# Weights handed over input dimension first in a graph and expert kernel

## The chip, the core and the metric
The program runs on one core of one Trainium2 chip as a single launch. The metric is the device time of that launch in microseconds (us); weights may be laid out in another order on the host before the launch, and that is not part of it. TensorE multiplies matrices, VectorE and ScalarE work elementwise, GpSimd issues the transfers that need an index per row (gathers and scatters) and SyncE issues the plain ones. Sixteen DMA engines carry both kinds. Each engine runs its own list of instructions in order, and semaphores are all that orders one list against another.

## The reference
The input is 6250 nodes of 512 numbers and 100000 edges (`src`, `dst`). Four layers follow each other, each on the layer-normalised result of the last and each added back to it: two narrow graph convolutions with a layer norm between them; a gated feed-forward layer with weights rounded to three levels; a third graph convolution; and 16 experts, one per token, chosen by a router.

```python
agg = segment_sum(x[src], dst); deg = maximum(segment_sum(1, dst), 1)     # third convolution
agg = agg / deg[:, None]
x3 = x + alpha * (agg @ W.T + b)                                          # W: 512 x 512
...
logits = xf @ switch_w.T + switch_b                                       # router, 16 x 512
probs = softmax(logits); routes = argmax(probs); route_probs = max(probs)
pos = running count of the route so far;  capacity = int(1.2 * N / 16)    # 468
buf[routes, pos] = xf                                                     # where pos < capacity
y = einsum('ecd,efd->ecf', buf, expert_w) + expert_b                      # expert_w: 16 x 512 x 512
out = where(pos < capacity, y[routes, pos], xf) * route_probs
```

All three weights (`W`, `switch_w`, `expert_w`) stand with the output dimension first. The product sums over the input dimension, and TensorE sums over the 128 partitions of its two operands, so it needs both with the input dimension on the partitions.

## The kernel before, in words
The program has four stages one after the other, with a barrier between them. The first sorts out edges, the second prepares tables, the third does the first two convolutions and the feed-forward layer, and the fourth, which is the one changed (from L1764 on), does the third convolution, the router and the experts. In every stage each engine has one function that issues its instructions in a written-out order (`@block.tensor`, `@block.scalar` and so on).

*Head of the fourth stage.* SyncE loads `Wg` into `wg`, the router's weights into `sw` (16 partitions of 512) and some small things. TensorE turns `Wg` in four groups of four 128x128 transposes into PSUM (L2081), and ScalarE copies each group into `wgT` (L2261); four more transposes and a copy make `swT`. Meanwhile VectorE clears 29 of 49 blocks of the sums `agg` (L2399), and ScalarE the rest. `wg` serves afterwards as the space of two other tiles (`scaled`, `xf`).

*Third convolution.* GpSimd gathers rows of the edges by unit (L1971); VectorE builds one-hot matrices (L2435); TensorE sums rows into nodes (L2122); ScalarE scales; TensorE turns the sums (L2140) and multiplies by `wgT` (L2150). Layer norm, logits (L2170) and routing tables follow a few tiles behind in the same loop.

*Experts.* Each of 16 experts has 468 slots, in tiles of 128, 128, 128 and 84 rows: 64 tiles, numbered f. For a tile, GpSimd has gathered the rows (`gather`, L1979) two experts ahead into `er`; ScalarE normalises them into `xe` (L2331); TensorE turns them (`turn_rows`, L2206); ScalarE rounds the turned rows to the narrower fp32 format of TensorE into `erT` (L2338), and VectorE keeps the remainder (L2552). The product (L2217) takes 12 matmuls of 512 columns: high part times high part, remainder times high, high times remainder, over four blocks of 128 inputs. VectorE adds the bias (L2595) and the scaled residual (L2597), and GpSimd scatters the result to `out` (L1996). The expert's weights go the same way as the rows: loaded into `we` (two buffers, L2043), turned (`turn_weights`, L2198) into `pWT`, rounded by ScalarE (`copy_weights`, L2325) and split by VectorE (`weights_rest`, L2547) into `weT`. While tile m of expert e is multiplied, block m of the weights of expert e+1 goes through these steps. In TensorE's order that is, per tile: rows of the next tile, a block of the next expert's weights, the product of this tile.

*What holds what.* SyncE loads the weights of expert e over those of e-2 when TensorE has turned the latter (L2069), and its next bias when the tiles of e-2 are finished (`biased`); both waits stand in one list. Before the first scatter, GpSimd waits for seven last blocks of `out` that SyncE stores after the gather of expert 0 has landed (L1993, L2065).

Of the kernel before, what the change touches and what calls it, by code (L numbers as in the profile page):

```python
# [4 lines left out]
F32 = mybir.dt.float32  # L5
# [11 lines left out]
P = 128  # L17
N = 6250
D = 512
DK = D // P  # L20
# [49 lines left out]
NX = 16  # L70
# [297 lines left out]
def program(nc, x, src, dst, node_vec, W1, b1, gamma, beta, W2, b2, w_gate, w_up, w_down,  # L368
            alpha, Wg, bg, switch_w, switch_b, expert_w, expert_b, out):
    with ExitStack() as whole:  # L370
# [889 lines left out]
        with ExitStack() as ctx:  # L1260
# [507 lines left out]
            "loaded loads const bg3 wT_ps wT scaled aT_ps aT conv res x3 var std rs xf xT_ps xT logits lg_done lg expd onehot cum placed "  # L1768
# [4 lines left out]
        es = {n: sem("e_" + n) for n in "wT_ps wT wT_lo xe xT_ps xT xT_lo y_ps biased y".split()}  # L1773
# [6 lines left out]
        with ExitStack() as ctx:  # L1780
# [18 lines left out]
            wg = sb(ctx, "wg", [P, DK, D], F32)  # L1799
# [9 lines left out]
            scaled, xf = wg[:, 0:2, :], wg[:, 2:4, :]  # L1809
# [3 lines left out]
            sw = aT[0:NX, 0].rearrange("p a b -> p (a b)")  # L1813
# [30 lines left out]
            pWT = [pb(ctx, f"pWT{j}", [P, DK, P], F32) for j in range(2)]  # L1844
# [159 lines left out]
            def _(sp):  # L2004
                sp.dma_start(wg[:], Wg.rearrange("(m p) d -> p m d", p=P)).then_inc(s["w_in"], 16)
                sp.dma_start(res[0:3, 0, :], bg.partition_broadcast(3)).then_inc(s["bias_in"], 16)
                sp.dma_start(alp[:], alpha.partition_broadcast(P)).then_inc(s["small_in"], 16)
                sp.dma_start(sw, switch_w).then_inc(s["small_in"], 16)
# [33 lines left out]
                def load_weights(e):  # L2042
                    sp.dma_start(we[:, e % 2, :, :], expert_w[e].rearrange("(m p) d -> p m d", p=P)).then_inc(ew_in[e % 2], 16)  # L2043
# [24 lines left out]
                for e in range(2, NX):  # L2068
                    sp.wait_ge(es["wT_ps"], (e - 1) * DK)  # L2069
                    load_weights(e)  # L2070
                    sp.wait_ge(es["biased"], (e - 1) * ET)
                    load_bias(e)

            @block.tensor
            def _(pe):
                pe.wait_ge(s["w_in"], 16)
                for c in range(DK):
                    if c > 0:
                        pe.wait_ge(s["wT"], c)
                    for m in range(DK):  # L2080
                        last = nc.tensor.transpose(pW[:, m * P:(m + 1) * P], wg[:, m, c * P:(c + 1) * P], ident[:])  # L2081
                    last.then_inc(s["wT_ps"], 1)
                pe.wait_ge(s["small_in"], 48)
                for c in range(DK):
                    last = nc.tensor.transpose(pT[:, 0, c * NX:(c + 1) * NX], sw[:, c * P:(c + 1) * P], ident[0:NX, 0:NX])
                last.then_inc(s["wT_ps"], 1)
                pe.wait_ge(s["wT"], DK + 1)
# [55 lines left out]
                def convolve(i, k):  # L2143
                    T = i * G + k
                    if isinstance(i, int) and T == 0:
                        pe.wait_ge(s["bg3"], 1)
                    wait_alone(pe, s["aT"], T + (1 + FREE), s["fence_pe"])
                    wait_alone(pe, s["x3"], T + FREE, s["fence_pe"])
                    for c in range(DK):
                        nc.tensor.matmul(pW[:], aT[:, k % 2, c, :], wgT[:, c, :], start=(c == 0), stop=False)  # L2150
                    nc.tensor.matmul(pW[:], tri[0:3, 1, :], bg3[:], start=False, stop=True).then_inc(s["conv"], 1)
# [40 lines left out]
                def turn_weights(e, c):  # L2192
                    if c == 0:
                        pe.wait_ge(ew_in[e % 2], (e // 2 + 1) * 16)
                    if e * DK + c >= 2:
                        pe.wait_ge(es["wT_lo"], e * DK + c - 1)
                    for m in range(DK):
                        last = nc.tensor.transpose(pWT[c % 2][:, m, :], we[:, e % 2, m, c * P:(c + 1) * P], ident[:])  # L2198
                    last.then_inc(es["wT_ps"], 1)

# [39 lines left out]
                turn_weights(0, 0)  # L2240
                turn_weights(0, 1)
                fill(G - 1, None)
                turn_weights(0, 2)
                turn_weights(0, 3)
                turn_rows(*experts[0])
                for f, e, m, n in experts:
                    if f + 1 < len(experts):
                        turn_rows(*experts[f + 1])
                    if e + 1 < NX:
                        turn_weights(e + 1, m)  # L2250
                    product(f, e, m, n)

            @block.scalar
            def _(act):
# [4 lines left out]
                for c in range(DK):  # L2259
                    act.wait_ge(s["wT_ps"], c + 1)  # L2260
                    nc.scalar.copy(wgT[:, c, :], pW[:]).then_inc(s["wT"], 1)  # L2261
                act.wait_ge(s["wT_ps"], DK + 1)
                nc.scalar.copy(swT[:].rearrange("p a b -> p (a b)"), pT[:, 0, 0:DK * NX]).then_inc(s["wT"], 1)

# [121 lines left out]
            def _(dve):  # L2386
# [248 lines left out]

_INS = ['x', 'src', 'dst', 'node_vec1', 'L0_gnn_W1', 'L0_gnn_b1', 'L0_gnn_gamma', 'L0_gnn_beta', 'L0_gnn_W2',
# [21 lines left out]
```

## Time and profile before

| what | value |
|---|---|
| median of 3 timed runs | 3362.64 us (3353.38 to 3371.6) |
| profiled execution, first to last instruction (its span) | 5135.2 us |
| mean granted clock of TensorE in it | 0.765 of full speed |
| fourth stage in it | from 3387.3 us |
| routing of the last tiles, between convolution and experts | about 4842 to 4894 us |
| experts (first to last product) | 4894.4 to 5128 us |
| busy, TensorE / VectorE / ScalarE / GpSimd | 2982.4 / 1973.4 / 1285.4 / 2000.5 us |

The profiled execution lies far above the timed ones; its own time is known as its span only. In the rows below PE is TensorE (its matmuls and transposes) and PEld its loading of the stationary operand, DVE is VectorE, ACT ScalarE, POOL GpSimd and SPq the transfers that SyncE issues. A timeline row gives the start in us from the beginning of the span, the duration in us, engine, line and operation, what is written and read with its shape, the number of instructions run together, and in brackets how long the engine was idle before and what ended that ("issue" means that nothing seen in the profile did). A row of a group ends with busy us and mean ns of one, and the idle time before. A row of a stretch gives from:to, its length, the busy us and number of instructions of PE, PEld, DVE, ACT and POOL, the granted clock, the DMA engines' busy share and GB/s. A row of a tile gives the count, the shortest, median and longest duration in ns, and the first and last start.

### The profile page before, as it was taken

What the parts mean: (1) busy time and instruction counts of PE and PEld (TensorE: products, weight loads), DVE (VectorE), ACT (ScalarE), POOL (GpSimd) and SP (SyncE); (2) the same over time, 40 slices, a digit from 0 to 9 for tenths busy, and PEclk for the clock granted to TensorE, in tenths of its full rate; (3) what the DMA queues carried; (4) which work ended last, traced back from release to release, by engine and by line L of the source; (5) the groups of instructions that cost most, each with busy time, mean ns of one, the idle gap of its engine ahead of it and who ended that gap; (6) DMA issues with size and microseconds to landing.
All of it is one profiled execution on the core that took longest, in us unless ns stands there. A gap on an engine that the chain in (4) does not pass through costs nothing. (4 is left out here: it accounts for less than half of the span.)

```text
span 5135.2 us, 61590 instructions
## 1 busy us (share of the span) xinstructions
PE 2982.4 (58%) x17153; PEld 2061.9 (40%) x17154; DVE 1973.4 (38%) x3813; ACT 1285.4 (25%) x2086; POOL 2000.5 (39%) x2038
## 2 busy tenths in 40 slices
PE   7511179631111000299989999956667666665789
PEld 7400068620000000177777777732232232322477
DVE  9300079750000000166666566632223223232366
ACT  3200057410000000144444444420011111111344
POOL 0377700037777777300000000035555455554244
PEclk9555589755555555599999999977888788887799
DMA  3101023210000000022333233345555556555465
GB/s 101 39 5 11 4 64 96 61 41 3 3 3 3 3 3 3 6 91 88 107 95 102 88 104 100 100 151 168 168 170 161 163 173 182 170 161 158 134 193 155
DMA packets 241523, 466.48 MB, mean 91 GB/s; under 512 B 77093, under 2 KB 107069, under 8 KB 241235
## 3 DMA queue, kind: packets, MB, share of 16 engines
q0 software_dynamic: 107264, 235.06, 17.4%
q1 hardware_dynamic: 133970, 227.93, 14.2%
q8 instruction: 138, 2.26, 0.2%
q14 instruction: 151, 1.23, 0.1%
HBM read 395.90 MB, written 73.45 MB: 91 GB/s over the span
## 5 line engine op out<-in xcount | busy, mean ns | idle before, releaser
L1971 POOL DMA_INDIRECT rows<-xn_rows,srcT x784 | 744.2, 949 | 665.4 <-DVEq L2441 440.7
L129 POOL DMA_INDIRECT msg_c<-hid_rows,srcT x744 | 770.0, 1035 | 245.0 <-issue 236.5
L2122 PE MATMUL pV<-rows,oh 128*128 x2240 | 645.5, 435 | 331.6 <-issue 262.2
L2122 PEld LDWEIGHTS pV<-rows,oh 128*128 x2240 | 238.7, 107 | 724.1 <-issue 576.2
L1197 PE MATMUL pG<-parts,los 128*128 128x200 bf16 x2640 | 308.6, 258 | 322.7 <-issue 322.7
L1487 PE MATMUL gates<-xT,wgu_hi 128*128 128x384 f32 (+1 forms) x1848 | 472.3, 377 | 39.2 <-ACT gate_sum L1585 20.6
L1954 POOL IOTA bases<- 128x49 f32 x1 | 0.2, 188 | 1269.8 <-POOLq L387 1269.8
L1518 PE MATMUL accs<-wd,hT 128*128 128x512 f32 x1617 | 405.4, 398 | 16.2 <-DVE hT L1733 16.2
L129 POOL DMA_INDIRECT msg_b<-hid_rows,srcT x344 | 345.5, 1004 | 110.2 <-issue 105.6
L1197 PEld LDWEIGHTS pG<-parts,los 128*128 128x128 bf16 x2640 | 240.9, 100 | 356.0 <-issue 354.2
L1487 PEld LDWEIGHTS gates<-xT,wgu_hi 128*128 128x128 f32 x1848 | 336.4, 190 | 105.4 <-issue 60.9
L1518 PEld LDWEIGHTS accs<-wd,hT 128*128 128x128 f32 x1617 | 303.5, 189 | 88.1 <-issue 28.4
L2435 DVE SCALAR_TENSOR_TENSOR oh<-ids,bases,dstT 128x896 f32 x160 | 184.1, 1150 | 401.4 <-issue 375.8
L2423 DVE TENSOR_TENSOR agg<-agg,pV x161 | 110.1, 684 | 547.9 <-PE pV L2122 348.2
L994 DVE TENSOR_REDUCE picked<-pG 128x32 f32<-128x800 f32 x110 | 108.5, 987 | 462.2 <-remote 359.4
L1433 PE MATMUL accs<-parts_c,los_c 128*128 128x200 bf16 x168 | 47.7, 323 | 305.0 <-issue 304.9
L2273 ACT ACTIVATE wg<-agg,invdeg 128x512 f32 (+1 forms) x49 | 35.3, 721 | 701.7 <-DVEq L118 578.6
L2150 PE MATMUL pW<-wgT,aT 128*128 128x512 f32 x392 | 197.4, 651 | 18.8 <-issue 12.6
L2217 PE MATMUL pY<-weT,erT 128*128 128x512 f32 (+1 forms) x768 | 193.7, 401 | 3.2 <-DVE weT L2547 2.2
L1637 DVE TENSOR_REDUCE msg_c<-accs 128x32 f32<-128x800 f32 x7 | 6.9, 991 | 485.2 <-remote 485.2
L1467 PE MATMUL accs<-w2b,aggT 128*128 128x512 f32 x8 | 8.2, 1125 | 290.1 <-issue 162.2
L1346 POOL MEMSET msg_c<- 128x152 f32 x1 | 0.2, 225 | 447.8 <-POOLq L387 447.8
(432 smaller groups left out, 5300.1 us busy)
## 6 DMA issues: line engine op xcount, KB each, us to landing
wd<-wd_rows SPq DMA_DIRECT2D x154, 512.0 KB
we<-in_L_ffn_expert_w SPq DMA_DIRECT2D x16, 1024.0 KB
lo<-lo_rows SPq DMA_DIRECT2D x110, 128.0 KB
x_rows<-xr SPq DMA_DIRECT2D x49, 256.0 KB, 4.0
xn_rows<-pair SPq DMA_DIRECT2D x49, 256.0 KB
rows<-xn_rows,srcT POOLq DMA_INDIRECT x784
res<-x_rows SPq DMA_DIRECT2D x49, 256.0 KB
x_rows<-agg SPq DMA_DIRECT2D x49, 256.0 KB
```

The lines of the kernel that those rows point to most:

```text
L129: nc.gpsimd.indirect_dma_start(msg[:, c, :], None, table, bass.IndirectOffsetOnAxis(ap=srcT[:, c:c + 1], axis=0)).then_inc(landed[u % 2], 16)
L994: nc.vector.tensor_reduce(picked[:, g // MB % 2, 4 * (g % MB):4 * (g % MB) + 4, :].rearrange("p (b c) f -> p b (c f)", b=2), pG[g % AHEAD] ...
L1197: last = nc.tensor.matmul(into, los[:, g % AHEAD, b, k * P:(k + 1) * P], parts[:, j, b].rearrange("p f h -> p (f h)"), start=False, stop=( ...
L1433: last = nc.tensor.matmul(into, los[:, g % AHEAD, b, k * P:(k + 1) * P], parts[:, j, b].rearrange("p f h -> p (f h)"), start=False, stop=( ...
L1487: last = nc.tensor.matmul(ps[:, 0:n], w, v, start=(m == 0), stop=(m == len(terms) - 1))
L1518: last = nc.tensor.matmul(acc4[j][:], h, wd[:, slot, w, :], start=(f == 0 and m == 0), stop=(f == FB - 1 and m == 2))
L1971: nc.gpsimd.indirect_dma_start(rows[:, u % RING, c, :], None, xn2_rows, bass.IndirectOffsetOnAxis(ap=srcT[:, u * Q + c:u * Q + c + 1], axi ...
L2122: last = nc.tensor.matmul(pV[:, ds(to, 1), :].rearrange("p a d -> p (a d)"), oh[:, ds(to, 1), c, :].rearrange("p a d -> p (a d)"), rows[:, ...
L2150: nc.tensor.matmul(pW[:], aT[:, k % 2, c, :], wgT[:, c, :], start=(c == 0), stop=False)
L2217: last = nc.tensor.matmul(pY[f % 2][0:n, :], erT[:, f % 2, j, c, 0:n], weT[:, e % 2, k, c, :], start=(j, k, c) == terms[0], stop=(j, k, c) ...
L2423: nc.vector.tensor_tensor(at, at, pV[:, ds((v + 1) % 2, 1), :].rearrange("p a b -> p (a b)"), ALU.add).then_inc(s["added"], 1)
L2435: nc.vector.scalar_tensor_tensor(oh[:, ds(v % 2, 1)].rearrange("p a q n -> p (a q) n"), bc(ids.unsqueeze(1), (P, Q, P)), bases[:, ds(tile, ...
```

## The change
The host hands over `W` and `switch_w` transposed and `expert_w` with its last two dimensions exchanged. SyncE loads the first two straight into `wgT` and `swT` (the latter now 128 partitions with four runs of 16 numbers each), and the head of the stage has no transposes and no copies of them. The space of `wg` remains as `between`, and the PSUM of `pWT` remains reserved. In the experts `turn_weights` is gone: ScalarE rounds from `we` itself and waits for its load, VectorE takes the remainder from `we`, and SyncE waits for VectorE's remainder before it loads over a buffer. TensorE's waits for the two loads of the head stand before its first convolution.

```diff
@@ SyncE, head and experts
-                sp.dma_start(wg[:], Wg.rearrange("(m p) d -> p m d", p=P)).then_inc(s["w_in"], 16)
+                sp.dma_start(wgT[:], WgT.rearrange("(c p) d -> p c d", p=P)).then_inc(s["w_in"], 16)
-                sp.dma_start(sw, switch_w).then_inc(s["small_in"], 16)
+                sp.dma_start(swT[:], switch_wT.rearrange("(c p) n -> p c n", p=P)).then_inc(s["small_in"], 16)
-                    sp.dma_start(we[:, e % 2, :, :], expert_w[e].rearrange("(m p) d -> p m d", p=P)).then_inc(ew_in[e % 2], 16)
+                    sp.dma_start(we[:, e % 2, :, :], expert_wT[e].rearrange("(c p) d -> p c d", p=P)).then_inc(ew_in[e % 2], 16)
                 for e in range(2, NX):
-                    sp.wait_ge(es["wT_ps"], (e - 1) * DK)
+                    sp.wait_ge(es["wT_lo"], (e - 1) * DK)
                     load_weights(e)
@@ TensorE, head
-                pe.wait_ge(s["w_in"], 16)
-                for c in range(DK):
-                    if c > 0:
-                        pe.wait_ge(s["wT"], c)
-                    for m in range(DK):
-                        last = nc.tensor.transpose(pW[:, m * P:(m + 1) * P], wg[:, m, c * P:(c + 1) * P], ident[:])
-                    last.then_inc(s["wT_ps"], 1)
...
-                pe.wait_ge(s["wT"], DK + 1)
                 pe.wait_ge(s["const"], 1)
                 pe.wait_ge(s["added"], 1)
@@ TensorE, convolve
                     if isinstance(i, int) and T == 0:
                         pe.wait_ge(s["bg3"], 1)
+                        pe.wait_ge(s["w_in"], 16)
+                        pe.wait_ge(s["small_in"], 48)
@@ TensorE, experts
-                def turn_weights(e, c):
-                    if c == 0:
-                        pe.wait_ge(ew_in[e % 2], (e // 2 + 1) * 16)
-                    if e * DK + c >= 2:
-                        pe.wait_ge(es["wT_lo"], e * DK + c - 1)
-                    for m in range(DK):
-                        last = nc.tensor.transpose(pWT[c % 2][:, m, :], we[:, e % 2, m, c * P:(c + 1) * P], ident[:])
-                    last.then_inc(es["wT_ps"], 1)
...
                 for f, e, m, n in experts:
                     if f + 1 < len(experts):
                         turn_rows(*experts[f + 1])
-                    if e + 1 < NX:
-                        turn_weights(e + 1, m)
                     product(f, e, m, n)
@@ ScalarE, experts
                 def copy_weights(e, c):
-                    act.wait_ge(es["wT_ps"], e * DK + c + 1)
+                    if c == 0:
+                        act.wait_ge(ew_in[e % 2], (e // 2 + 1) * 16)
                     if e >= 2:
                         act.wait_ge(es["y_ps"], (e - 1) * ET)
-                    nc.scalar.copy(weT[:, e % 2, 0, c, :], pWT[c % 2][:].rearrange("p a b -> p (a b)")).then_inc(es["wT"], 1)
+                    nc.scalar.copy(weT[:, e % 2, 0, c, :], we[:, e % 2, c, :]).then_inc(es["wT"], 1)
@@ VectorE, experts
-                    nc.vector.tensor_tensor(weT[:, e % 2, 1, c, :], pWT[c % 2][:].rearrange("p a b -> p (a b)"),
+                    nc.vector.tensor_tensor(weT[:, e % 2, 1, c, :], we[:, e % 2, c, :],
@@ host
+TURNED = {'L1_gnn_W': (1, 0), 'L1_ffn_switch_w': (1, 0), 'L1_ffn_expert_w': (0, 2, 1)}
```

On TensorE, at the border between the last but one and the last expert, these instructions stand in the order of before (`pWT` is the PSUM of the turned weights, `pXT` that of the turned rows, `pY` the product):

```order
L2206 MATMUL pXT<-ident,xe 128x128 x4
L2198 MATMUL pWT<-ident,we 128x128 x4
L2217 MATMUL pY<-weT,erT 84x512 x12
L2206 MATMUL pXT<-ident,xe 128x128 x4
L2217 MATMUL pY<-weT,erT 128x512 x12
```

and in the changed one:

```order
L2186 MATMUL pXT<-ident,xe 128x128 x4
L2197 MATMUL pY<-weT,erT 84x512 x12
L2186 MATMUL pXT<-ident,xe 128x128 x4
L2197 MATMUL pY<-weT,erT 128x512 x12
```

The four transposes of the weights are gone from every tile of the first 15 experts; the last expert had none before. On TensorE between routing and the first product stood (`pS` takes the counts and tables of the routing):

```order
L2179 MATMUL pS<-oh16b,tri 128x112 x2
L2198 MATMUL pWT<-ident,we 128x128 x8
L2186 MATMUL pS<-names,slot 128x128 x7
L2198 MATMUL pWT<-ident,we 128x128 x8
L2206 MATMUL pXT<-ident,xe 128x128 x8
L2198 MATMUL pWT<-ident,we 128x128 x4
L2217 MATMUL pY<-weT,erT 128x512 x12
```

and now stands:

```order
L2168 MATMUL pS<-oh16b,tri 128x112 x2
L2175 MATMUL pS<-names,slot 128x128 x7
L2186 MATMUL pXT<-ident,xe 128x128 x8
L2197 MATMUL pY<-weT,erT 128x512 x12
```

Twenty transposes are gone there; ScalarE and VectorE keep their instructions in their places and read `we` in place of `pWT`.

## Rows read from the trace of the kernel before

**Rows 1.** The page's costliest groups, TensorE's sums of the third convolution.
```profile
L2122 PE MATMUL pV<-rows,oh 128*128 x2240 | 645.5, 435 | 331.6 <-issue 262.2
```

**Rows 2.** Busy time by stretch, middle of the experts.
```profile
5000.00:5050.00 50.00, 50.00 (x280) 41.01 (x279) 35.95 (x57) 24.75 (x42) 27.69 (x28) 1.00 0.69 200
```

**Rows 3.** Timeline, TensorE's weight loads over one tile.
```profile
5004.29 0.58 PEld L2206 LDWEIGHTS pXT<-ident,xe 128*128 128x128 f32 x4
5004.85 0.47 PEld L2198 LDWEIGHTS pWT<-ident,we 128*128 128x128 f32 x4
5005.28 2.60 PEld L2217 LDWEIGHTS pY<-weT,erT 128*128 128x128 f32 x12
...
5007.92 0.52 PEld L2206 LDWEIGHTS pXT<-ident,xe 84*128 84x128 f32 x4
```

**Rows 4.** Timeline, the same in the last expert.
```profile
5115.74 0.59 PEld L2206 LDWEIGHTS pXT<-ident,xe 128*128 128x128 f32 x4
...
5118.94 0.59 PEld L2206 LDWEIGHTS pXT<-ident,xe 128*128 128x128 f32 x4
```

**Rows 5.** Timeline, start of the experts, up to tile 8.
```profile
4909.71 1.03 POOL L1996 DMA_INDIRECT out<-ye,index  x1 [12.48 <-issue]
...
4911.27 0.65 PE L2198 MATMUL pWT<-ident,we 128*128 128x128 f32 x4 [0.71 <-DMA we<-in_L_ffn_expert_w]
...
4919.94 0.82 ACT L2331 ACTIVATE xe<-er 128x512 f32<-128x512 f32 x1 [3.71 <-DMA er<-x_rows,index]
...
4921.40 0.59 PEld L2206 LDWEIGHTS pXT<-ident,xe 128*128 128x128 f32 x4
...
4929.78 2.99 PE L2217 MATMUL pY<-weT,erT 128*128 128x512 f32 x12 [2.15 <-DVE weT L2547]
```

**Rows 6.** Instructions on the tile pWT.
```profile
L2325 ACT CAST weT<-pWT x64: 586/594/607, 4874.6 to 5113.5; 128x512 fp32r<-128x512 f32 x64
L2547 DVE TENSOR_TENSOR weT<-pWT,weT x64: 675/679/692, 4885.0 to 5114.6; 128x512 fp32r<-128x512 f32 x64
```

**Rows 7.** Timeline of the third stage, a remainder out of SBUF.
```profile
3383.04 0.69 DVE L1754 TENSOR_TENSOR pair<-xn,pair 128x512 f16<-128x512 f32 x1 [2.45 <-ACT pair L1615]
```

**Rows 8.** Timeline, VectorE and GpSimd over one tile.
```profile
5001.13 0.69 DVE L2595 TENSOR_TENSOR ye<-pY,be 84x512 f32<-84x512 f32 x1 [0.95 <-issue]
5001.15 0.97 POOL L1981 DMA_INDIRECT er<-x_rows,index  x1 [0.30 <-issue]
...
5001.85 0.75 DVE L2597 SCALAR_TENSOR_TENSOR ye<-ye,er 84x512 f32<-84x512 f32 x1
...
5003.12 0.68 DVE L2547 TENSOR_TENSOR weT<-pWT,weT 128x512 fp32r<-128x512 f32 x1
...
5004.77 0.69 DVE L2595 TENSOR_TENSOR ye<-pY,be 128x512 f32<-128x512 f32 x1 [0.97 <-issue]
```

**Rows 9.** Timeline, SyncE's issue of an expert's weights.
```profile
5002.22 0.44 SPq L2043 DMA_DIRECT2D we<-in_L_ffn_expert_w  x1
```

**Rows 10.** Busy time by stretch, ten microseconds after that load.
```profile
5012.50:5013.00 0.50, 0.50 (x5) 0.34 (x4) 0.47 (x2) 0.50 (x2) 0.50 (x1) 1.00 0.01 0
```

**Rows 11.** SyncE's waits: total us, times, longest us.
```profile
SPq L2046 <- DVE ye L2595: 176.2, 13, 18.5
...
SPq L118 <- DMA x_rows<-tok: 4.2, 2, 2.1
```

**Rows 12.** Timeline, head of the fourth stage.
```profile
3392.16 12.43 DVE L2399 MEMSET agg<- 128x14848 f32 x1 [3.16 <-issue]
...
3405.24 0.21 ACT L2263 COPY swT<-pT 128x64 f32<-128x64 f32 x1 [1.01 <-issue]
...
3412.75 1.15 DVE L2435 SCALAR_TENSOR_TENSOR oh<-ids,bases,dstT 128x896 f32 x1 [3.05 <-issue]
```

**Rows 13.** Instructions on the tile ye, 4930 to 5115 us.
```profile
L2597 DVE SCALAR_TENSOR_TENSOR ye<-ye,er x52: 746/752/753, 4930.3 to 5113.3; 128x512 f32<-128x512 f32 x39, 84x512 f32<-84x512 f32 x13
```

**Rows 14.** Instructions on the tile er, 4930 to 5115 us.
```profile
L1981 POOL DMA_INDIRECT er<-x_rows,index x50: 956/976/1276, 4930.6 to 5105.5; - x50
```

More of the change, by code:

```diff
@@ L368, in program @@
 def program(nc, x, src, dst, node_vec, W1, b1, gamma, beta, W2, b2, w_gate, w_up, w_down,
-            alpha, Wg, bg, switch_w, switch_b, expert_w, expert_b, out):
+            alpha, WgT, bg, switch_wT, switch_b, expert_wT, expert_b, out):
     with ExitStack() as whole:
@@ L1767, in program @@
             "w_in small_in bias_in fence fence_sp fence_pe fence_dve fence_act rows_ready rows_used oh_ready mm_done added whole "
-            "loaded loads const bg3 wT_ps wT scaled aT_ps aT conv res x3 var std rs xf xT_ps xT logits lg_done lg expd onehot cum placed "
+            "loaded loads const bg3 scaled aT_ps aT conv res x3 var std rs xf xT_ps xT logits lg_done lg expd onehot cum placed "
             "mapped map_ps map_free z tok_out tok_free indexed blank cleared dve pool".split())}
@@ L1772, in program @@
         o_out = [sem(f"d_o_out{k}") for k in range(G)]
-        es = {n: sem("e_" + n) for n in "wT_ps wT wT_lo xe xT_ps xT xT_lo y_ps biased y".split()}
+        es = {n: sem("e_" + n) for n in "wT wT_lo xe xT_ps xT xT_lo y_ps biased y".split()}
         ew_in = [sem(f"e_w_in{j}") for j in range(2)]
@@ L1798, in program @@
             bases = sb(ctx, "bases", [P, NT], F32)
-            wg = sb(ctx, "wg", [P, DK, D], F32)
+            between = sb(ctx, "between", [P, 4, D], F32)
             wgT = sb(ctx, "wgT", [P, DK, D], F32)
@@ L1808, in program @@
             tri = sb(ctx, "tri", [P, 2, P], BF16)
-            scaled, xf = wg[:, 0:2, :], wg[:, 2:4, :]
+            scaled, xf = between[:, 0:2, :], between[:, 2:4, :]
             aT = sb(ctx, "aT", [P, 2, DK, P], F32)
@@ L1812, in program @@
             res = sb(ctx, "res", [P, 3, D], F32)
-            sw = aT[0:NX, 0].rearrange("p a b -> p (a b)")
             rs1 = sb(ctx, "rs1", [P, NT], F32)
@@ L1843, in program @@
             sums_banks.close()
-            pWT = [pb(ctx, f"pWT{j}", [P, DK, P], F32) for j in range(2)]
+            pb(ctx, "rest_of_visits", [P, 2, D], F32)
             pXT = [pb(ctx, f"pXT{j}", [P, DK, P], F32) for j in range(2)]
@@ L2075, in _ @@
             def _(pe):
-                pe.wait_ge(s["w_in"], 16)
-                for c in range(DK):
-                    if c > 0:
-                        pe.wait_ge(s["wT"], c)
-                    for m in range(DK):
-                        last = nc.tensor.transpose(pW[:, m * P:(m + 1) * P], wg[:, m, c * P:(c + 1) * P], ident[:])
-                    last.then_inc(s["wT_ps"], 1)
[L2083 to L2086, printed above, removed]
-                pe.wait_ge(s["wT"], DK + 1)
                 pe.wait_ge(s["const"], 1)
@@ L2239, in _ @@
                 cumulate(G - 1, None)
-                turn_weights(0, 0)
-                turn_weights(0, 1)
                 fill(G - 1, None)
-                turn_weights(0, 2)
-                turn_weights(0, 3)
                 turn_rows(*experts[0])
@@ L2258, in _ @@
                 act.sem_inc(s["cleared"], 1)
[L2259 to L2263, printed above, removed]
                 for n in ("aT", "xT", "res"):
@@ L2648 @@
     for name in _INS:
-        a = np.ascontiguousarray(inputs[name])
+        a = np.asarray(inputs[name])
+        a = np.ascontiguousarray(np.transpose(a, TURNED[name]) if name in TURNED else a)
         if a.ndim == 0:
```

## The prediction
> **What bounds the kernel now.** I read the page's costliest groups first, and they give a warning. The largest idle time of TensorE belongs to the sums of the third convolution, and is put down to "issue", not to another engine [rows 1]. The profiled span is 5135.2 us where the timed median is 3362.64 us, so some 1770 us of the profile are not in the timed runs, and idle time of that kind, in a stage of loops and register work, is where I look for them. The change barely touches that stage. It touches the experts, from about 4894 us to the end, so I read next the table by stretches: from 5000 to 5050 us TensorE is busy 50 of 50 us at a granted clock of 1.00 (2.4 GHz), while VectorE is busy 35.95, ScalarE 24.75 and the DMA engines 0.69 of the time [rows 2]. That stretch has no idle time in which the two kinds of run could differ, so I subtract microseconds found there from the timed median as they stand.
>
> The timeline of TensorE's weight loads in that stretch shows one tile of tokens: turning the rows starts at 5004.29, turning the weights at 5004.85, the product at 5005.28, and the next tile's rows at 5007.92 [rows 3]. So a tile takes 3.63 us, of which 5.28 - 4.85 = 0.43 us are the four transposes that the change drops. The kernel holds its own trial of the dropped work: the last expert has no successor whose weights must be turned, and there the tiles are 5118.94 - 5115.74 = 3.20 us apart [rows 4]. The difference is 0.43 us again.
>
> The beginning of the experts is bound by something else. The first scatter of results waits 12.48 us on GpSimd and starts at 4909.71, as it must follow the landing of the last seven `out` blocks (L1993). The gathers for expert 2 queue behind it, and ScalarE waits 3.71 us, until 4919.94, for the first of them to land. TensorE turns those rows at 4921.40. It also waits 0.71 us for the weights of expert 2, and at 4929.78, before the first product of expert 2 (tile 8), 2.15 us for VectorE [rows 5]. No transpose of weights lies in this chain from landing to gather to landing.
>
> **The change part by part.**
> Transposes in the expert loop. There are 15 experts with a successor times 4 tiles, 60 groups of four. Nine are issued before the product of tile 8, 51 after it. The 51 lie on a TensorE that is never idle: 51 x 0.43 = 21.9 us. The nine (3.9 us) and the two waits' weight part (0.71 us) stand in front of the DMA chain: TensorE reaches tile 8 earlier and waits there. The rows of tile 8 exist from 4919.94 + 0.82 = 4920.76 on, and TensorE took them at 4921.40, so 0.6 us can be had there at once, and a little more if the later wait shrinks. Bounds 0 and 4.6 us; I take 1, near the 0.6 that these rows show. Sum: 22.9 us.
>
> The copies that now read SBUF. ScalarE's rounding copy takes 586/594/607 ns from PSUM, VectorE's remainder 675/679/692 [rows 6]; a remainder of the same shape out of SBUF alone takes 0.69 us [rows 7], and ScalarE's normalising of that shape from SBUF, with scale and bias, 0.82 us [rows 5]. So 0.01 us per tile more on VectorE and at most 0.23 on ScalarE, beside TensorE. Cover: VectorE has per tile the bias (0.69), the scaled sum (0.75), the rows' remainder (0.68) and this one (0.68), from 5001.13 to 5003.80; its next bias starts at 5004.77 [rows 8], so 0.97 us are free, of which the shorter tile takes 0.43. If that cover were gone, 0.01 x 51 = 0.5 us would show. ScalarE, busy 24.75 of 50 [rows 2], has some 1.8 us per tile.
>
> The new wait of ScalarE for an expert's weights (TensorE waited before). Behind it on ScalarE queue the normalising of the rows two tiles ahead and the copy of the next tile's turned rows, for which VectorE and then TensorE's product wait. The weights are issued at 5002.22 [rows 9], and by 5012.5 the DMA engines are down to 0.01 busy [rows 10], so they land within 10.3 us. Needed they are one expert later: four tiles, 4 x 3.63 = 14.5 us now and 4 x 3.20 = 12.8 us after. So 2.5 us are left and the wait costs 0; were the landing later than that, TensorE would follow it.
>
> SyncE waits for VectorE's remainder instead of TensorE's transposes before it loads over the old weights. In front of that load stands the bias load, whose wait for the finished tiles ends last (176.2 us over 13 loads) [rows 11], and VectorE computes that remainder before it finishes the tile. Cost 0; without that cover, the 2.2 us from the transposes' end (5005.28 less a tile) to the remainder's, at 5003.80, paid from the 2.5 us above.
>
> Head of the stage. 20 transposes, four copies of 128x512 and one small copy go. They lie beside VectorE's clearing of the sums, which runs from 3392.16 for 12.43 us, and the first one-hot follows at 3412.75 [rows 12]; the transposes are in neither. Bounds 0 and 0.9 us (from the end of the clearing at 3404.59 to that of the last copy, for which TensorE waits too, at 3405.45); I take 0, since VectorE's row comes last. The convolution's new waits for the two loads are met long before. The router's weights now come as 512 pieces of 64 bytes; a store of 896 pieces of 16 bytes is waited for at most 2.1 us [rows 11], and this one has over 15 us. Cost 0.
>
> Between routing and experts, 16 transposes go that TensorE did while it waited for the routing tables and the first gather: 0. ScalarE's seven last `out` blocks can come 1 us earlier, but their store waits for the gather of expert 0: 0.
>
> Total: 22.9 us, so the profiled span goes from 5135.2 to about 5112, and the timed median from 3362.6 to 3339.7 us. What comes next is still TensorE: 3.20 us per tile against VectorE's 2.8.
>
> **A rule that speaks against the change.** VectorE's remainder of the weights used to read PSUM and SBUF; now both inputs are in SBUF, while GpSimd issues gathers and scatters. In this trace an instruction with two SBUF inputs, the scaled sum, already runs beside them: it starts at 5001.85 under a gather that began at 5001.15 and lasts 0.97 us, and takes 0.75 us [rows 8]. Over 52 tiles it takes 746/752/753 ns [rows 13], so VectorE was never held up. A gather took 956/976/1276 ns [rows 14]; at worst GpSimd gives way by 0.3 us, and it is busy 27.69 of 50 us [rows 2]. The Trainium skill (SBUF — State Buffer, Who interferes with whom) says that a VectorE instruction with two SBUF inputs and a GpSimd instruction that reads SBUF shut each other out, the later one waiting for the whole of the other. By that rule VectorE would wait up to one GpSimd instruction per tile; the trace agrees at most on GpSimd's side.
>
> **The rivals.**
> All of it comes through. If in a timed run the landings at the start of the experts are quicker, the nine groups count too, and the head's 0.9 us: 21.9 + 4.6 + 0.9 = 27.4 us, 3335.2 us. For it: the profiled run is the slower one throughout. Against: a wait of 12.48 us on landings is no small margin.
>
> The transfers take over. An expert moves the same bytes in 12.8 instead of 14.5 us, and the DMA engines, busy 0.69 now, would be busy 0.69 x 14.5 / 12.8 = 0.78. If the weights' landing stretches from 10.3 to past 12.8 us, ScalarE stalls every expert. With the period halfway, at 13.65 us, half of the gain is left: 3351 us. For it: at the start the gather behind the scatter of 4909.71 landed only at 4919.94. Against: the quiet at 5012.5.
>
> Slower: VectorE becomes the bound through the shut-out. Its place is the remainder of the weights. VectorE has 2.81 us of work per tile, so it decides from 3.63 - 2.81 = 0.82 us of waiting per tile. One wait of 0.98 us, a gather in full, makes 3.79 us, 51 x 0.16 = 8 us slower; two such 4.77 us, 51 x 1.14 = 58 us slower. Midway, 33 us: 3396 us. Against it: rows 8 and 13.
>
> **How the numbers follow.** Forecast 3339.7 us: 0.62, own range 3332 to 3347. All of it: 0.15. The transfers: 0.16. Slower: 0.07. The spread of the three timed runs (3353.38 to 3371.6) widens each case by several microseconds. From 3327 to 3356 less than two in ten are left out. What a measurement can tell from no change is about 0.5%, 16.8 us. Forecast and full gain pass it nearly always, each losing about a tenth to the spread: faster 0.70. The transfers and that tenth: same 0.23. Slower 0.07, most of the last rival and little else.
>
> **What would show it.** Right: the groups of transposes into the weights' PSUM tiles are gone, TensorE stays 50 of 50 busy at 1.00 in the middle of the experts, tiles follow each other in 3.20 us, an expert in about 12.7 us (one tile of the four is shorter), and the first product of expert 2 still starts near 4929 us on a span's scale that is otherwise unchanged. VectorE's scaled sum and remainder keep 0.75 and 0.69 us. Wrong: ScalarE waits for the weights' DMA in every expert; VectorE's four instructions stretch or start late beside GpSimd; the granted clock falls inside the experts; or the stage before 4840 us, which holds the greater part of the time, moves by more than the experts do.

## The result, and the profile after

The changed kernel takes 3343.6 us (median of 20 runs, 3330.2 to 3354.3) against 3364.5 us of the kernel before: a ratio of 0.9937, interval 0.9925 to 0.995. That is 20.9 us less, between 17 and 25. The forecast was 3339.7 us, 22.9 us less.

The profiled execution of the changed kernel has a span of 3332.8 us and is not stretched as the one of before was. TensorE's sums of the third convolution are idle 148.7 us where [rows 1] had 331.6. First the page's group, then busy time by stretch in the middle of the experts (us busy and instructions of PE, PEld, DVE, ACT, POOL, then granted clock, DMA share, GB/s), which answer to [rows 1, 2]:

```profile
L2109 PE MATMUL pV<-rows,oh 128*128 x2240 | 553.6, 395 | 148.7 <-issue 50.2
```

```profile
3150.00:3200.00 50.00, 50.00 (x254) 39.73 (x253) 40.93 (x64) 28.21 (x48) 34.19 (x32) 1.00 0.76 249
...
3250.00:3300.00 50.00, 50.00 (x255) 39.81 (x253) 40.90 (x65) 28.32 (x48) 33.98 (x32) 1.00 0.69 213
```

TensorE is still busy 50 of 50 us at a clock of 1.00 (2.4 GHz), so it still sets the pace. The others are busier per stretch because more tiles fit into it, and GpSimd also because its scatters take longer (below). The timeline of TensorE's weight loads shows one tile, as [rows 3] did:

```profile
3300.70 0.59 PEld L2186 LDWEIGHTS pXT<-ident,xe 128*128 128x128 f32 x4
3301.26 2.60 PEld L2197 LDWEIGHTS pY<-weT,erT 128*128 128x128 f32 x12
3303.90 0.59 PEld L2186 LDWEIGHTS pXT<-ident,xe 128*128 128x128 f32 x4
```

3303.90 - 3300.70 = 3.20 us instead of 3.63; the group on the weights' PSUM tiles is gone. The instructions that write the weights' tile (least/median/greatest ns), which answer to [rows 6], read SBUF now:

```profile
L2294 ACT CAST weT<-we x64: 601/623/627, 3093.2 to 3311.5; 128x512 fp32r<-128x512 f32 x64
L2516 DVE TENSOR_TENSOR weT<-we,weT x64: 673/683/693, 3106.4 to 3312.7; 128x512 fp32r<-128x512 f32 x64
```

GpSimd's scatters and gathers, by least/median/greatest ns, answer to [rows 14]:

```profile
L1980 POOL DMA_INDIRECT er<-x_rows,index x64: 940/975/1477, 3107.2 to 3305.0; - x64
L1995 POOL DMA_INDIRECT out<-ye,index x64: 958/1149/1270, 3131.5 to 3328.4; - x64
```

The start of the experts, which answers to [rows 5], went otherwise than forecast. In order of time: the first scatter, ScalarE's copy of expert 2's weights, VectorE's bias of tile 4, ScalarE's rows of tile 8; then TensorE's products of tiles 6, 7 and 8.

```profile
3131.49 1.02 POOL L1995 DMA_INDIRECT out<-ye,index  x1 [12.52 <-DVE ye L2566]
3133.07 0.62 ACT L2294 CAST weT<-we 128x512 fp32r<-128x512 f32 x1 [2.46 <-DMA we<-in_L_ffn_expert_w]
3138.16 0.69 DVE L2564 TENSOR_TENSOR ye<-pY,be 128x512 f32<-128x512 f32 x1 [3.74 <-DMA out<-ye,index]
3138.65 0.81 ACT L2300 ACTIVATE xe<-er 128x512 f32<-128x512 f32 x1 [3.25 <-DMA er<-x_rows,index]
```

```profile
3115.60 2.93 PE L2197 MATMUL pY<-weT,erT 128*128 128x512 f32 x6
...
3140.29 5.49 PE L2197 MATMUL pY<-weT,erT 128*128 128x512 f32 x12 [4.06 <-DVE erT L2521]
3145.58 0.85 PE L2186 MATMUL pXT<-ident,xe 128*128 128x128 f32 x4
3146.18 3.03 PE L2197 MATMUL pY<-weT,erT 128*84 128x512 f32 x12
3149.05 0.60 PE L2186 MATMUL pXT<-ident,xe 128*128 128x128 f32 x4
3149.41 0.94 PE L2197 MATMUL pY<-weT,erT 128*128 128x512 f32 x3
```

TensorE waits 4.06 us before tile 6. VectorE's remainder of the rows of that tile stands behind its bias of tile 4, which waits for the first scatter to land and free its buffer. Then twelve matmuls that take 3.0 us elsewhere take 5.49. The stretches say why (granted clock third from the end):

```profile
3135.00:3140.00 5.00, 1.24 (x9) 0.86 (x7) 1.81 (x3) 1.75 (x4) 3.78 (x5) 0.92 0.88 335
3140.00:3145.00 5.00, 4.71 (x11) 3.75 (x12) 3.21 (x6) 1.03 (x2) 3.78 (x5) 0.50 0.39 123
```

After the wait the granted clock is 0.50 (1.2 GHz). From the product of tile 0, at 3115.60, to that of tile 8, at 3149.41, 33.8 us pass.

### The profile page after: what moved, and what is told of

Its sections match the earlier page's. It is cut to its first block and busy times, and to the rows that moved or that the text cites. A ratio compares the mean times of both kernels' runs of the same rounds, so it can differ in the third digit from the quotient of the medians.

```text
span 3332.8 us, 60976 instructions
## 1 busy us (share of the span) xinstructions
PE 2722.5 (82%) x16877; PEld 1976.2 (59%) x16878; DVE 1977.9 (59%) x3813; ACT 1281.7 (38%) x2081; POOL 2023.7 (61%) x2038
## 5 line engine op out<-in xcount | busy, mean ns | idle before, releaser
L129 POOL DMA_INDIRECT msg_c<-hid_rows,srcT x744 | 751.2, 1010 | 239.3 <-issue 226.2
L2109 PE MATMUL pV<-rows,oh 128*128 x2240 | 553.6, 395 | 148.7 <-issue 50.2
L129 POOL DMA_INDIRECT msg_b<-hid_rows,srcT x344 | 379.0, 1102 | 112.5 <-issue 105.8
L1518 PEld LDWEIGHTS accs<-wd,hT 128*128 128x128 f32 x1617 | 304.3, 190 | 88.3 <-issue 28.3
L1197 PE MATMUL pG<-parts,los 128*128 128x200 bf16 x2640 | 274.0, 252 | 0.0
L2241 ACT ACTIVATE between<-agg,invdeg 128x512 f32 (+1 forms) x49 | 35.3, 721 | 553.7 <-DVEq L118 553.7
L2197 PE MATMUL pY<-weT,erT 128*128 128x512 f32 (+1 forms) x768 | 195.7, 404 | 4.1 <-DVE erT L2521 4.1
L1591 ACT ACTIVATE up_sum<-gates,wscale 128x512 f32<-128x512 f32 (+1 forms) x154 | 97.6, 634 | 218.7 <-PE gates L1487 218.6
L1723 DVE SCALAR_TENSOR_TENSOR up_sum<-pU,wscale,up_sum 128x512 f32<-128x512 f32 (+1 forms) x154 | 105.1, 682 | 127.0 <-ACT up_sum L1591 122.9
L1487 PE MATMUL gates<-xT,wgu_lo 128*128 128x512 f32 (+1 forms) x462 | 172.3, 373 | 0.0
L1717 DVE SCALAR_TENSOR_TENSOR gate_sum<-gates,wscale,gate_sum 128x512 f32<-128x512 f32 (+1 forms) x154 | 105.4, 684 | 111.5 <-PE gates L1487 76.7
L1487 PE MATMUL pU<-xT,wgu_hi 128*128 128x512 f32 (+1 forms) x616 | 162.6, 386 | 6.1 <-DVE up_sum L1723 6.1
```

The costliest lines, as they stand in the source:

```text
L129: nc.gpsimd.indirect_dma_start(msg[:, c, :], None, table, bass.IndirectOffsetOnAxis(ap=srcT[:, c:c + 1], axis=0)).then_inc(landed[u % 2], 16)
L1197: last = nc.tensor.matmul(into, los[:, g % AHEAD, b, k * P:(k + 1) * P], parts[:, j, b].rearrange("p f h -> p (f h)"), start=False, stop=( ...
L1487: last = nc.tensor.matmul(ps[:, 0:n], w, v, start=(m == 0), stop=(m == len(terms) - 1))
L1518: last = nc.tensor.matmul(acc4[j][:], h, wd[:, slot, w, :], start=(f == 0 and m == 0), stop=(f == FB - 1 and m == 2))
L1717: nc.vector.scalar_tensor_tensor(gate_sum[:, 0:n], pG[1][:, 0:n], wscale[:, f, 1:2], gate_sum[:, 0:n], ALU.mult, ALU.add).then_inc(s["gate ...
L1723: nc.vector.scalar_tensor_tensor(up_sum[:, 0:n], pU[0][:, 0:n], wscale[:, FB + f, 0:1], up_sum[:, 0:n], ALU.mult, ALU.add).then_inc(s["up_ ...
```

## The experiments

Two numbers are read from each trace: from the product of tile 0 to that of tile 8 (the start), and from there to the last tile's, number 63 (the rest). A product is twelve matmuls, so these are the starts of its first one on TensorE's timeline. Ratios are to the kernel before; a kernel run once has only a trace.

| kernel | ratio (interval) | start | rest |
|---|---|---|---|
| before, first profile | | 35.3 | 195.7 |
| before, again | | 31.4 | 195.7 |
| changed | 0.9937 (0.9925 to 0.995) | 33.8 | 173.7 |
| changed, again | 0.9960 (0.9941 to 0.9979) | 29.0 | 173.6 |
| experts only | 0.9947 (0.9929 to 0.9965) | 34.3 | 173.7 |
| head only | 0.9999 (0.9981 to 1.0018) | 31.3 | 195.7 |
| 51 transposes' groups back | 1.0012 (0.9993 to 1.0031) | 33.9 | 195.7 |
| first nine groups back | | 31.3 | 173.7 |
| wait filled | | 31.6 | 173.7 |
| remainder twice | 0.9943 (0.9925 to 0.9962) | 33.5 | 175.0 |
| gathers first and two sets | 0.9918 (0.9902 to 0.9934) | 28.3 | 173.7 |
| the same again | 0.9928 (0.9901 to 0.9954) | 28.7 | 173.7 |
| gathers first | | 34.8 | 173.7 |
| two sets | | 28.6 | 173.6 |

**Which part carries the gain.** Experts only: the kernel before with the edits of the change on the experts alone. Head only: the change without them.

```diff
-TURNED = {'L1_gnn_W': (1, 0), 'L1_ffn_switch_w': (1, 0), 'L1_ffn_expert_w': (0, 2, 1)}
+TURNED = {'L1_ffn_expert_w': (0, 2, 1)}                          # experts only
+TURNED = {'L1_gnn_W': (1, 0), 'L1_ffn_switch_w': (1, 0)}         # head only
```

> The kernel before, with only the weights of the experts handed over with the input dimension first; the third convolution's and the router's weights are still turned on TensorE. Theory A (the gain is TensorE's time per tile of the experts, 51 groups of transposes x 0.43 us, and the head is worth nothing): the whole difference of the changed kernel, about -21 us against the kernel before, 3343 us or so. Theory B (part of the 21 us comes from the head, up to its 0.9 us, or from a shift of everything behind it): at least some microseconds less than that, 3350 us or more. In the profile A expects tiles 3.20 us apart and a stretch from the first to the last product of the experts near 210 us, as in the changed kernel.

> The changed kernel, with the weights of the experts turned on TensorE as before; only the third convolution's and the router's weights are handed over turned. Theory A (the head is hidden beside VectorE's clearing of the sums): 0 us against the kernel before, at most -1. Theory B (the head or the stage behind it carries part of the gain): -5 us or more. In the profile both expect tiles 3.63 us apart in the experts.

Experts only gives 0.9947 and the same 173.7 us for the rest; head only gives 0.9999. Theory A holds: the intervals leave the head some microseconds of room either way. The trace leaves it less: from the clearing of the sums to the first one-hot it is 2035.83 - 2015.26 = 20.57 us in the changed kernel, and 2049.51 - 2028.95 = 20.56 in the one before.

```profile
2015.26 12.43 DVE L2368 MEMSET agg<- 128x14848 f32 x1 [3.16 <-issue]
2035.83 1.15 DVE L2404 SCALAR_TENSOR_TENSOR oh<-ids,bases,dstT 128x896 f32 x1 [3.05 <-issue]
```

```profile
2028.95 12.43 DVE L2399 MEMSET agg<- 128x14848 f32 x1 [3.16 <-issue]
2049.51 1.15 DVE L2435 SCALAR_TENSOR_TENSOR oh<-ids,bases,dstT 128x896 f32 x1 [3.06 <-issue]
```

**The transposes put back, late and early.** The condition is `9 <= f < 60` for the 51 groups and `f < 9` for the nine.

```diff
                         turn_rows(*experts[f + 1])
+                    if 9 <= f < 60:
+                        for j in range(DK):
+                            nc.tensor.transpose(pWT[m % 2][:, j, :], weT[:, e % 2, 0, m, j * P:(j + 1) * P].bitcast(F32), ident[:])
                     product(f, e, m, n)
```

> The changed kernel with four transposes put back for each tile from tile 9 to tile 59, 51 groups; they read the weights in use and write a PSUM tile that nothing reads, so no copy and no wait comes back. Theory A (TensorE's time alone): +51 x 0.43 = +21.9 us against the changed kernel, so about the time of the kernel before, within 3 us. Theory C (reading SBUF in both inputs costs VectorE, ScalarE or GpSimd time, which takes part of what TensorE gained): slower than the kernel before by several microseconds, since the copies still read SBUF. In the profile A expects 3.63 us per tile.

> The changed kernel with four transposes put back for each of tiles 0 to 8, nine groups, read and written as in the kernel with 51 groups. Theory A (the early tiles stand in front of a chain of transfers, so that what TensorE saves there is waited for): from the first product of the experts to the product of tile 8 at most 1.5 us longer than the 33.8 us of the changed kernel, and nothing that the median would show. Theory B (they count as the others do): 9 x 0.43 = 3.9 us longer, 37.7 us.

With the 51 groups the rest is 195.7 us again, 22.0 more, and the time that of the kernel before; copies that read SBUF cost nothing that shows. So the gain is TensorE's own time. With the nine early groups both theories fell: the start became not longer but 2.5 us shorter than in the changed kernel. There TensorE, held back by the transposes, waits 1.31 us before tile 7 instead of 4.06 before tile 6, and no product is slow after it.

```profile
3159.68 2.99 PE L2197 MATMUL pY<-weT,erT 128*84 128x512 f32 x12 [1.31 <-DVE erT L2524]
```

**The kernel before once more.**

> The kernel before, profiled once more, since its first profile had a span of 5135.2 us against a median of 3364 us. Theory A (its profile was stretched in the third convolution, and at the start of the experts too): a span near 3360 us, and from the first product of the experts to that of tile 8 near 31.3 us, as in the kernel in which only the head was changed, not the 35.3 us that the first profile showed. Theory B (35.3 us is what this kernel takes there): 35 us again; the change would then have gained 1.5 us there.

Theory A: a span of 3367.3 us, 148.1 us of idle time before the sums of the third convolution instead of the 331.6 of [rows 1], and a start of 3161.86 - 3130.51 = 31.4 us.

```profile
3130.51 2.06 PE L2217 MATMUL pY<-weT,erT 128*128 128x512 f32 x4
...
3161.86 3.01 PE L2217 MATMUL pY<-weT,erT 128*128 128x512 f32 x12
```

So the stretch of [rows 5] was disturbed too, by 3.9 us, and the early term of the forecast was worked out there. Against this profile the changed kernel's start was 2.4 us longer.

**The wait filled.**

```diff
+                    if f == 6:
+                        for j in range(32):
+                            nc.tensor.transpose(pWT[j // DK % 2][:, j % DK, :], weT[:, e % 2, 0, m, j % DK * P:(j % DK + 1) * P].bitcast(F32), ident[:])
                     product(f, e, m, n)
```

> The changed kernel with 32 transposes into a PSUM tile that nothing reads, all of them in front of the product of tile 6, where TensorE waits 4.06 us and after which the granted clock stands at 0.5 for 6.8 us. Theory A (the clock falls after that wait, and the slow products of tiles 6 and 7 are what the start of the experts loses): with the wait filled (32 x 0.108 = 3.4 us) the clock stays at 1.00, the product of tile 6 takes about 3.0 instead of 5.49 us, and tile 8's product starts 31 us after tile 0's instead of 33.8. Theory B (the transfers alone set tile 8's place): 33.8 us again, whatever the clock.

```profile
3140.44 3.66 PE L2227 MATMUL pWT<-ident,weT 128*128 128x128 f32 x32
3144.89 3.06 PE L2197 MATMUL pY<-weT,erT 128*128 128x512 f32 x12 [0.79 <-DVE erT L2524]
```

```profile
3140.00:3145.00 5.00, 4.21 (x39) 3.88 (x38) 2.21 (x4) 1.66 (x3) 3.78 (x5) 1.00 0.92 340
```

Theory A: tile 6 came no earlier (25.1 us after tile 0, against 24.7), but its product took 3.06 us, the granted clock stayed at 1.00, and tile 8 stands 2.2 us earlier. So two things ate the early groups' gain: the later landing took it back (31.6 us here against 31.4 in the kernel before), and the fall of the clock cost 2.2 us on top.

**An earlier start.** Two sets of result buffers (`ye`, with a semaphore for each set), and the four gathers of expert 2 ahead of the wait for the last `out` blocks; then each edit alone.

```diff
-            ye = sb(ctx, "ye", [P, ET, D], F32)
+            ye = sb(ctx, "ye", [P, 2 * ET, D], F32)
...
+                for m in range(ET):
+                    pool.wait_ge(es["y"], m + 1)
+                    gather(2, m)
                 for k in range(G):
                     pool.wait_ge(o_out[k], G * 16)
...
-                    if e + 2 < NX:
+                    if 0 < e < NX - 2:
                         gather(e + 2, m)
...
-                    if e > 0:
-                        dve.wait_ge(e_out[m], e * 16)
+                    if e > 1:
+                        dve.wait_ge(e_out[e % 2 * ET + m], e // 2 * 16)
```

> The changed kernel with two edits at the start of the experts: GpSimd gathers the rows of expert 2 before it waits for the last out blocks, and the results have two sets of buffers, so that VectorE doesn't wait for the first scatter's landing. Theory A (TensorE there waits only for the landings behind the out blocks): the wait of 4.06 us and the fall of the clock go, tile 8's product starts some 28 us after tile 0's instead of 33.8, and the median is about 6 us under the changed kernel's, some 27 us under that of the kernel before. Theory B (the earlier gathers share the DMA engines with the out blocks and the weights of expert 2, which then land later): 32 us or more, no gain in the median.

> Only the first of the two edits: GpSimd gathers the rows of expert 2 before it waits for the last out blocks; the results keep one set of buffers. Theory A (VectorE's wait for the first scatter's landing holds TensorE up by itself, since the remainder of tile 6's rows stands behind it on VectorE): tile 6 starts 24 us or more after tile 0, the clock falls, and tile 8 starts 33 us or more after it. Theory B (the wait for the gather is what counts): tile 8 at 28 to 30 us.

> Only the second of the two edits: two sets of buffers for the results; the gathers of expert 2 stay behind the wait for the out blocks. Theory A (the gather behind the scatter is the next wait, 0.5 us later than the scatter's landing in the changed kernel): ScalarE still waits some 3 us for the rows of tile 8, TensorE waits one or two tiles later than before, and tile 8 starts 30 to 33 us after tile 0. Theory B (the scatter's landing is the only wait): 28 us.

The first scatter's landing is the wait that counts: two sets alone give 28.6 us, gathers first alone 34.8, with 5.52 us of waiting and a slow product again. With both it is 28.3, theory A. Two sets alone did better than the 30 to 33 us expected: the wait for the gather is there (4.84 us on ScalarE) but costs TensorE only 1.20.

```profile
3140.72 0.66 PE L2186 MATMUL pXT<-ident,xe 128*128 128x128 f32 x4 [1.20 <-ACT xe L2300]
```

**Is that version faster than the changed kernel?** Both were timed again, on one chip.

> The changed kernel once more, beside the version with an earlier start on the same chip. Both theories expect its earlier ratio, 0.9937, and from the first product to that of tile 8 again 33.8 us, with a fall of the clock.

> The changed kernel with the gathers of expert 2 in front of the wait for the last out blocks, and two sets of buffers for the results, timed again beside the changed kernel. Its trace had 204.5 us from first to last product against 210.0. Theory A (those 5.5 us are real in the median): a ratio 0.0016 under the changed kernel's. Theory B (they come back elsewhere, as in the stage before, which differs by some 15 us from run to run): the same ratio as the changed kernel.

The medians say 0.9928 against 0.9960, but the intervals overlap, as they do for the first pair (0.9918 and 0.9937); the points agree, the difference is not settled. The trace of the changed kernel shows one reason why it is hard to see. Against what both theories expected, its start was 29.0 us this time, not 33.8: VectorE waited 2.25 us for the scatter's landing instead of 3.74, TensorE 1.18 instead of 4.06, and the clock did not fall.

```profile
3139.06 0.69 DVE L2564 TENSOR_TENSOR ye<-pY,be 128x512 f32<-128x512 f32 x1 [2.25 <-DMA out<-ye,index]
```

```profile
3141.19 3.02 PE L2197 MATMUL pY<-weT,erT 128*128 128x512 f32 x12 [1.18 <-DVE erT L2521]
3144.05 0.60 PE L2186 MATMUL pXT<-ident,xe 128*128 128x128 f32 x4
3144.84 2.99 PE L2197 MATMUL pY<-weT,erT 128*84 128x512 f32 x12 [0.19 <-DVE erT L2521]
```

So the start has two outcomes, 5 us apart. Four of the five traces that keep the changed kernel's start (changed, experts only, 51 groups back, remainder twice) show the long one.

What goes with the two is the place of another transfer, the load of expert 3's weights (1024 KB). SyncE issues it behind the bias load of expert 2, which waits until tile 3 has its bias, so it follows TensorE's pace. The first scatter is held by the `out` blocks instead. Here are the first scatter, that load and VectorE's bias of tile 4, and for the kernel before also the bias of tile 5; first the kernel before, again:

```profile
3145.19 1.02 POOL L1996 DMA_INDIRECT out<-ye,index  x1 [12.01 <-issue]
3146.84 0.46 SPq L2043 DMA_DIRECT2D we<-in_L_ffn_expert_w  x1
3150.26 0.69 DVE L2595 TENSOR_TENSOR ye<-pY,be 128x512 f32<-128x512 f32 x1 [1.51 <-PE pY L2217]
3156.29 0.69 DVE L2595 TENSOR_TENSOR ye<-pY,be 128x512 f32<-128x512 f32 x1 [3.36 <-DMA out<-ye,index]
```

then the first nine groups back:

```profile
3146.61 1.02 POOL L1995 DMA_INDIRECT out<-ye,index  x1 [11.54 <-issue]
3147.94 0.43 SPq L2042 DMA_DIRECT2D we<-in_L_ffn_expert_w  x1
3150.47 0.69 DVE L2567 TENSOR_TENSOR ye<-pY,be 128x512 f32<-128x512 f32 x1 [0.96 <-PE pY L2197]
```

the changed kernel again, whose bias of tile 4 is shown above:

```profile
3133.92 1.03 POOL L1995 DMA_INDIRECT out<-ye,index  x1 [11.69 <-issue]
3134.53 0.43 SPq L2042 DMA_DIRECT2D we<-in_L_ffn_expert_w  x1
```

and the load in the changed kernel's first profile, whose scatter and bias stand in the result:

```profile
3130.75 0.43 SPq L2042 DMA_DIRECT2D we<-in_L_ffn_expert_w  x1
```

Where TensorE still turns the early weights (before, head only, nine groups back), the load comes 1.3 to 1.7 us behind the scatter, and the bias of tile 4 waits for TensorE alone; it is tile 5's bias that waits for a scatter. In the changed kernel's second profile the load comes 0.61 us behind it, and the bias starts 5.1 us after the scatter's issue. In the four long traces the load stands between 0.74 us ahead of the scatter and 0.12 us behind it, and 6.7 to 7.7 us pass. So the shorter tiles bring a large load forward onto the scatter that TensorE will wait for. No run moved the load alone, so this order is read from the traces, and not shown by an experiment of its own.

**VectorE's cover.**

```diff
+                    dve.wait_ge(es["spared"], e * DK + c)
+                    nc.vector.tensor_tensor(spare[:], we[:, e % 2, c, :],
+                                            weT[:, e % 2, 0, c, :].bitcast(F32), ALU.subtract).then_inc(es["spared"], 1)
                     nc.vector.tensor_tensor(weT[:, e % 2, 1, c, :], we[:, e % 2, c, :],
```

> The changed kernel in which VectorE computes the remainder of the weights twice, the first time into a spare tile; both read two SBUF inputs beside GpSimd's gathers and scatters. VectorE then has 2.81 + 0.69 = 3.50 us of work for a full tile, against TensorE's 3.20. Theory A (VectorE isn't held up by GpSimd, and had about half a microsecond per tile to spare): the remainder still takes 0.69 us, tiles are about 3.5 us apart, between +6 and +17 us against the changed kernel. Theory B (instructions with two SBUF inputs and GpSimd shut each other out): the remainder or the scaled sum takes 1 us and more, tiles are 3.8 us apart or more, over +30 us, slower than the kernel before.

```profile
3200.00:3250.00 50.00, 49.98 (x253) 39.48 (x251) 49.18 (x80) 28.36 (x48) 40.53 (x32) 1.00 0.73 230
```

```profile
3237.21 0.68 DVE L2518 TENSOR_TENSOR spare<-we,weT 128x512 f32<-128x512 f32 x1
3237.81 0.68 DVE L2520 TENSOR_TENSOR weT<-we,weT 128x512 fp32r<-128x512 f32 x1
3238.41 0.69 DVE L2568 TENSOR_TENSOR ye<-pY,be 128x512 f32<-128x512 f32 x1
```

VectorE is busy 49.18 of 50 us and TensorE is hardly held up: the rest is 1.3 us longer, the ratio 0.9943. Theory B is out: the remainder keeps 0.68 us, the scaled sum a median of 0.75. Theory A had the mechanism, and its size was too large: instructions of 0.68 us start 0.60 us apart, so durations added up overstate VectorE's work per tile. GpSimd pays instead. First the kernel before, again, then this one:

```profile
L1996 POOL DMA_INDIRECT out<-ye,index x64: 959/1017/1112, 3145.2 to 3362.9; - x64
...
L1996 POOL DMA_INDIRECT out<-ye,index x64: 957/1512/1762, 3136.9 to 3335.8; - x64
```

The median scatter took 1017 ns in the second profile of before (one VectorE instruction with two SBUF inputs per tile), 1149 in the changed kernel (two), 1512 here (three). The shorter tiles are not the reason: with the 51 groups back, at the pace of before, it is 1149 too. TensorE does not wait for it.

## Why the prediction was right, and where not

**The 51 groups: right, and sized right.** Forecast 51 x 0.43 = 21.9 us; measured 195.7 - 173.7 = 22.0, on the stretch from tile 8 to the end. Taking them away gave it, and putting them back took it.

**The nine early groups: wrong.** The step that failed is "TensorE reaches tile 8 earlier and waits there", with its bounds of 0 and 4.6 us and the 1 us taken, and with it the premise that no transpose of weights lies in the chain of landings. The transposes set when tile 3 is finished, and so when the load of expert 3's weights is issued: without them, by the order in the traces, it came up against the first scatter, which in the first profile held VectorE's bias of tile 4 for 3.74 us, where in the kernel before that bias waited for no transfer. The step also gave waiting no price. Where TensorE's wait grew to 4 us, the granted clock fell to 0.50, and the start came out 2.4 us longer than the 31.4 us of the kernel before; where the landing came sooner (1.18 us of waiting), 2.3 us shorter. A loss had been left out of the bounds. The sign was hidden also because [rows 5] stood in a disturbed stretch, which showed 35.3 us. The forecast named a fall of the clock inside the experts as what would prove it wrong, and in four of the five traces that keep the changed kernel's start it fell, once in each. The Trainium skill (TensorE: Matmul & The Clock Gate, HAM oscillation — how this bites in real kernels) describes a TensorE that waits for transfers and then starts again at the slower level. The trace agrees: 0.50 after 4.06 us, 1.00 after 1.18.

**The place of the wait.** The forecast looked for what comes late at the landing of the gather (ScalarE's 3.71 us in [rows 5]). The edit of one part at a time shows the landing of the first scatter, through VectorE's bias of tile 4, as the one that holds TensorE.

**The head: right.** 0 of up to 0.9 us: 20.57 us against 20.56.

**The copies out of SBUF: right.** VectorE's remainder takes 683 for 679 ns, its scaled sum 752 as before, ScalarE's rounding 623 for 594. VectorE's spare time per tile, forecast 0.97 - 0.43 = 0.54 us, is the 0.51 or 0.52 before its bias:

```profile
3239.90 0.68 DVE L2516 TENSOR_TENSOR weT<-we,weT 128x512 fp32r<-128x512 f32 x1
3241.09 0.69 DVE L2564 TENSOR_TENSOR ye<-pY,be 128x512 f32<-128x512 f32 x1 [0.52 <-issue]
```

**ScalarE's and SyncE's new waits: right but for one.** ScalarE waited for weights once in the experts, 2.46 us at the start, where the load stands behind the `out` blocks; in the thirteen later loads never. The wait of SyncE in front of the load is still the bias load's. That the load of expert 3 then comes earlier was priced at nothing; by the order in the traces, that is where the loss at the start began.

**The transfers** were busier, 0.69 to 0.76, near the 0.78 of the rival, but with no wait for weights that rival had no price.

**The slower rival** is refuted by the run with a third such instruction: VectorE was not held up, GpSimd was: its median scatter grew by 0.13 us in the changed kernel, within the 0.3 us that the forecast allowed it. By the rule of the Trainium skill (SBUF — State Buffer, Who interferes with whom) either engine would wait where the other came first; the runs show it on GpSimd's side alone.

**The sum.** By the traces 22.0 + 0 with a start of -2.4 or +2.3 us makes 19.6 or 24.3; the medians say 20.9, between 17 and 25. The forecast of 22.9 lies inside because its large term was exact, and the wrong one was small; that the 1 us taken lies between the two outcomes of the start is luck. The second comparison of the same two kernels says 0.9960, 13 us less, between 7 and 20, and the forecast lies above that; why it is less there is not shown. The rival in which all of the early groups count, 4.6 us, was not seen: the best start of the changed kernel gained 2.3.

## What to carry to other kernels

Price removed work on the engine that is never idle, from the distance of two tiles with it and without it; here a last expert without the work gave the answer to 0.1 us in 22. Before taking work off TensorE in front of a landing, ask which transfers the faster engine will issue earlier, what they then stand in front of, and whether the clock survives the longer wait: such work can be worth keeping, or the landing should be moved out of the way (here a second set of result buffers). When a profile's span is far over the median, read the stretches that look healthy a second time in another profile before small terms are taken from them.

## What was not expected of the hardware

After 4.06, 4.23 and 5.52 us of waiting, TensorE's next product took 5.49, 5.49 and 5.08 us instead of 3.0, and the granted clock stood at 0.50; after 0.79, 1.18, 1.26 and 1.31 us, and after the 2.15 us of [rows 5], it stayed at 1.00. Nine groups of transposes that nothing needs made the start 2.5 us shorter.

The first product of the experts lies anywhere from 3115.6 to 3132.0 us into the profiled runs other than the first one of the kernel before, whichever version it is; that spread in front of the part that changed is a likely reason why 5 us are hard to see in a median.
